# A two-layer graph kernel on one core: own place tables for each engine and batch, and a ring of 16 tiles

## The reference

```python
h = relu(layernorm(x))
# layer 0: 4 heads of 32, keys in 8 chunks of 128, softmax WITHIN each chunk
q, k, v = h @ Wq.T + bq, h @ Wk.T + bk, h @ Wv.T + bv
scores = where(adj == 0, -10, clip(q k^T / sqrt(32), -10, 10))   # adj as [row, chunk, key]
ctx = sum over chunks of softmax(scores in chunk) @ v_chunk
x = x + layernorm(ctx @ Wo.T + bo + h) * gamma + beta
# layer 1: graph attention
h = relu(layernorm(x)); Wh = h @ W
e = leaky_relu(Wh @ a1 (rows) + Wh @ a2 (columns)), -inf where adj == 0 off the diagonal
x = x + elu(softmax(e) @ Wh)
```

## Time and profile before

| | us |
|---|---|
| median of 3 runs | 904.6 (904.54 to 905.9) |
| the profiled execution | 901.52 |
| its span | 899.7 |
| DVE busy | 762.5 (85%) |
| PE busy | 750.4 (83%) |
| ACT busy | 593.6 (66%) |
| POOL busy | 512.3 (57%) |

### The profile page before, as it was taken

How to read it: one execution, slowest core, us unless ns; L and a number is a source line. 1 busy time by engine, 2 the same in 40 slices (tenths; PEclk the granted TensorE clock), 3 DMA queues, 4 the chain that set the end, 5 groups by cost and what they waited for, 6 DMA issues and landing times.

```text
span 899.7 us, 14629 instructions
## 1 busy us (share of the span) xinstructions
PE 750.4 (83%) x5031; PEld 429.3 (48%) x5031; DVE 762.5 (85%) x1348; ACT 593.6 (66%) x940; POOL 512.3 (57%) x478
## 2 busy tenths in 40 slices
PE   4799999988898998898899998898899887754644
PEld 2334444344454544464455545464356435644543
DVE  4877887898989988998989899998989896786783
ACT  6686787876867587767768676767865685235242
POOL 1301453463866667655866567755855487867443
PEclk9699999999999999999999999999999999766868
DMA  8413224202311223121321142121231201010101
GB/s 271 150 71 117 71 83 141 83 24 83 124 65 55 81 94 107 59 77 42 129 87 50 66 147 70 54 82 61 70 100 38 75 14 34 19 53 24 38 4 35
DMA packets 58648, 68.58 MB, mean 76 GB/s; under 512 B 5328, under 2 KB 35024, under 8 KB 58576
## 3 DMA queue, kind: packets, MB, share of 16 engines
q1 hardware_dynamic: 57568, 67.39, 22.3%
q10 hardware_dynamic: 1008, 0.26, 0.1%
HBM read 21.50 MB, written 12.58 MB: 38 GB/s over the span
## 4 chain that ended last, share of the span: by engine, by line
DVE 41%; PE 28%; issue 13%; ACT 9%; POOL 7%; DMA 1%; DVEq 0%; POOLq 0%; SPq 0%; ACTq 0%
DVE probs L854 14%; PE work L993 10%; DVE ring L756 6%; DVE ring L782 5%; PE ctx_ps L1035 4%; PE score L1022 4%; PE sum_ps L1041 4%; PE work L915 3%; DVE small L717 3%; DVE scaled L748 3%; ACT score L649 2%; POOL ring L464 2%; DVE small L722 1%; POOL h L494 1%; DVE inverse L832 1%
## 5 line engine op out<-in xcount | busy, mean ns | idle before, releaser
L854 DVE SCALAR_TENSOR_TENSOR probs<-score,cap 128x1024 f32<-128x1024 f32 x256 | 307.8, 1211 | 27.6 <-ACT score L649 27.4
L649 ACT ACTIVATE score<-score 128x1024 f32<-128x1024 f32 x256 | 257.5, 1011 | 61.5 <-PE score L1022 60.0
L514 POOL TENSOR_TENSOR gathered<-gathered,scaled 128x512 f32<-128x512 f32 x112 | 150.0, 1339 | 147.4 <-DVE scaled L748 147.4
L1022 PE MATMUL score<-query_stack,key_stack 128*128 128x512 f32 x512 | 190.6, 455 | 41.3 <-DVE probs L854 39.9
L464 POOL TENSOR_TENSOR ring<-ring,see_t 128x512 f32<-128x512 f32 x112 | 138.2, 1243 | 50.7 <-DVE ring L782 50.7
L993 PE MATMUL work<-wh,ring 128*128 128x129 f32 x1024 | 131.6, 288 | 40.0 <-ACT ring L572 38.4
L993 PEld LDWEIGHTS work<-wh,ring 128*128 128x128 f32 x1024 | 127.6, 204 | 48.8 <-issue 45.0
L1035 PE MATMUL ctx_ps<-probs,value 128*32 128x512 f32 x1024 | 137.7, 610 | 0.7 <-ACT context L657 0.7
L1041 PE MATMUL sum_ps<-probs,one_of 128*32 128x512 f32 x1024 | 135.1, 600 | 0.0
L782 DVE SCALAR_TENSOR_TENSOR ring<-near_row,wh,to_row 128x512 f32<-128x512 f32 x128 | 107.2, 853 | 27.3 <-ACT to_row L629 20.9
L1022 PEld LDWEIGHTS score<-query_stack,key_stack 128*128 128x128 f32 x512 | 79.5, 192 | 94.5 <-DVE probs L854 77.6
(11 more groups left out here) (99 smaller groups left out, 894.6 us busy)
## 6 DMA issues: line engine op xcount, KB each, us to landing
query_stack<-query_parts SPq DMA_DIRECT2D x64, 256.0 KB, 2.5
key_stack<-key_parts SPq DMA_DIRECT2D x64, 256.0 KB, 2.6
x_in<-in_x SPq DMA_DIRECT2D x16, 256.0 KB, 3.5
h_kept<-x_in SPq DMA_DIRECT2D x16, 256.0 KB, 2.0
res<-h_kept SPq DMA_DIRECT2D x16, 256.0 KB, 2.7
h<-in_x SPq DMA_DIRECT2D x16, 256.0 KB, 3.2
x_kept<-res SPq DMA_DIRECT2D x16, 256.0 KB, 2.6
gat_x<-x_kept SPq DMA_DIRECT2D x32, 128.0 KB, 2.3
```

What stands on the lines that cost most here:

```text
L514: nc.gpsimd.tensor_tensor(gathered[:, :, :], gathered[:, :, :], scaled[:, :, :], ALU.add).then_inc(gathered_step, 1)
L649: nc.scalar.activation(some, some, ACT.Exp, scale=DH ** -0.5).then_inc(exp_done, 1)
L854: nc.vector.scalar_tensor_tensor(out=probs[:, step[2] % 2, h:h + GROUP, :], in0=score[:, h:h + GROUP, :], scalar=LOW, in1=caps.broadcast_t ...
L1022: last = nc.tensor.matmul(score[:, head, :], key_stack[:, head, sc * P:(sc + 1) * P], query_stack[:, head, sq * HALF:(sq + 1) * HALF], sta ...
```

## The change

- The one table of slots is replaced by tables of places, one for each engine, and in them one for each batch: `in_order(engine)` sorts `b * 9600 + place` and each engine issues in that order. Every piece has a place of its own on each engine that has a part in it (a job on PE, its reading on ACT or DVE, its sum on POOL).
- The ring has 16 tiles. The wait in the middle of a batch's leaky pieces is gone; each half waits for the last shares of that half of the batch before.
- The peaks write their scratch output to `near_row` in place of ring tiles 6 and 7.
- Norms are cut in pieces (stats, moments, shift), ELU too (invert, divide, below, above), context and sums on PE as well, each with its own place.
- Masks: the turned adjacency and the second weights pass through the two `work` banks, not the `score` banks; the first half's `probs` waits for 4 masks only (`masks_made`), the second half's for 8.
- x is loaded and waited for by halves, and some semaphores are split by half.

What is computed and the kinds and sizes of the instructions stay as they are. The diff, cut to its core:

```diff
-RING = 12
+RING = 16
-JOBS = {
-    "turn_x0": -49, "turn_x1": -39, "query0": -29, "key0": -26, "value0": -20, ...
-}
-AT = {
-    "load_x": [-79], "moments_x": [-62, -57], "rstd_x": [-63, -57], ...
-}
+PLACES = 9600
+TENSOR = ({}, {
+    0: {
+        "scores": [-45, 13, 169, 668, 910, 1088, 1771, 1894, 2362, 2565, 2568, 2912, ...
+def table_of(engine, b):
+    return {**ENGINES[engine][0], **ENGINES[engine][1].get(b, {})}
+def in_order(engine):
+    found = [(b * PLACES + place, name, k, b) for b in range(BATCHES)
+             for name, places in table_of(engine, b).items() for k, place in enumerate(places)
+             if name != "hide" or here(engine, b, k)]
+    return [item[1:] for item in sorted(found, key=lambda item: item[0])]
...
-                        if step == (0, 0, 0):
-                            dve.wait_ge(masks_made, CHUNKS)
+                        if b == 0 and step % CHUNKS == 0:
+                            dve.wait_ge(masks_made, TILES * (step // CHUNKS + 1))
...
-                if n == RING:
-                    dve.wait_ge(work_done[bank_of("share1", g)], count_of("share1", g))
+                        if b:
+                            used = ("share", half * TILES + TILES - 1, b - 1)
+                            dve.wait_ge(work_done[bank_of(*used)], count_of(*used))
...
-                    out=ring[:, SCRATCH:SCRATCH + 2, :].rearrange("p a n -> p (a n)"), in0=to_row[:, :], in1=see[:, t, :],
+                        out=near_row[:, :], in0=to_row[:, :], in1=see[:, k, :], scale=1.0, scalar=-3e38, op0=ALU.add,
...
-                        last = nc.tensor.transpose(adj_turned_ps(t)[:, jt * P:(jt + 1) * P],
+                        last = nc.tensor.transpose(work[:, bank, :].bitcast(BF16)[:, jt * P:(jt + 1) * P],
```

More of the change, by code:

```diff
@@ new lines, with turn_of, bank_of @@
+IN_WORK = ("turn_x", "query", "key", "value", "gather", "turn_sums", "turn_context", "project", "turn_hidden", "to_row",
+           "wh", "near_row", "base_row", "share", "mask", "weights")
+TURNS = [item for item in in_order("tensor") if item[0] in IN_WORK and not (item[0] == "share" and item[1] % PAIR)]
+TURN_OF = {item: n for n, item in enumerate(TURNS)}
+def turn_of(name, k, b):
+    return TURN_OF[name, k // PAIR * PAIR if name == "share" else k, b]
+def bank_of(name, k, b):
+    return turn_of(name, k, b) % 2
@@ L96, in live, with count_of @@
+def count_of(name, k, b):
+    return turn_of(name, k, b) // 2 + 1
 def live(g):
     return 0 <= g < BATCHES
[L100 to L106, removed]
[L109 to L126 removed]
@@ L129, in step_at, with here @@
-def step_at(i, n, after):
-    i, n = i + (n - after) // SLOTS, (n - after) % SLOTS
-    return [(i, n // PHASE, n % PHASE // HEADS)] if n % HEADS == 0 and live(i) else []
-def group_at(i, n, places):
-    i, n = i + (n + places) // SLOTS, (n + places) % SLOTS
-    return [((i, n // PHASE, n % PHASE // HEADS), n % HEADS)] if n % GROUP == 0 and live(i) else []
-def group(step, h, plus=0):
-    i, q, c = step
-    return i * GROUPS + ((q * CHUNKS + c) * HEADS + h) // GROUP + plus
-def number(step, plus=0):
-    i, q, c = step
-    return i * STEPS + q * CHUNKS + c + plus
+def here(engine, g, n):
+    return (n in HIDE_HERE.get(g, ())) == (engine == "vector")
@@ L153, in build, with hidden, step_of, group_of @@
+def hidden(engine, g, n):
+    return sum(here(engine, f, t) for f in range(g + 1) for t in range(2 * CHUNKS if f < g else n + 1))
+def step_of(b, k):
+    return b * STEPS + k
+def group_of(b, k):
+    return b * GROUPS + k
 def build(nc, x, adj, Wq, bq, Wk, bk, Wv, bv, Wo, bo, gamma, beta, W, a, out):
@@ L721, in moments @@
                 for t in range(TILES):
-                    last = nc.vector.bn_aggr(moment[:, t, :], stats[:, t, :])
+                    last = nc.vector.bn_aggr(norm[s][1][:, t, :], norm[s][0][:, t, :])
                 last.then_inc(moments_done[s], 1)
@@ L969, in job @@
                         last = nc.tensor.matmul(work[:, bank, n * WIDE:(n + 1) * WIDE], h1_t[:, t * P:(t + 1) * P],
                                                 w1[:, :], start=True, stop=True)
-                elif name.startswith("to_row"):
-                    wait_read(f"turn_hidden{half}", b)
-                    last = nc.tensor.matmul(work[:, bank, :], w1_a[:, 1:2].broadcast_to([P, P]), h1_t[:, side],
-                                            start=True, stop=True)
-                elif name.startswith("near_row") or name.startswith("base_row"):
-                    pe.wait_ge(peak_done, b * 2 + 2)
-                    kind = int(name.startswith("base"))
-                    for t in range(TILES):
-                        tile = half * TILES + t
-                        last = nc.tensor.transpose(work[:, bank, t * P:(t + 1) * P],
-                                                   row_shift[:, kind, tile:tile + 1].broadcast_to([P, P]), eye[:, :])
-                else:
-                    assert name.startswith("share"), name
-                    pe.wait_ge(gat_exp_done, b * 2 * CHUNKS + CHUNKS * (half // 2 + 1))
-                    share(b, half, 0)
-                    return
@@ L987, in job @@
-                last.then_inc(work_done[bank], 1)
-            def share(g, k, part):
-                bank = bank_of(f"share{k}", g)
-                half, t = k // 2, k % 2 * PAIR + part
-                for jt in range(CHUNKS):
-                    last = nc.tensor.matmul(work[:, bank, part * (1 + D):(part + 1) * (1 + D)],
-                                            ring[:, (half * CHUNKS + jt) % RING, t * P:(t + 1) * P], wh[:, jt, 0:1 + D],
-                                            start=jt == 0, stop=jt == CHUNKS - 1)
-                if part == PAIR - 1:
-                    last.then_inc(work_done[bank], 1)
```

1796 lines of the change are left out of this document (1262 added, 534 removed), and 14 rows, old and new, of tables (JOBS, READ_AFTER).

## The result

The changed kernel takes **854.1 us** (median of 4 runs, 853.23 to 856.08) against 904.6 us (904.03 to 905.9): ratio 0.944, 95% interval 0.9424 to 0.9463. Forecast were 877 us and a range of 859 to 895. The direction was right and the size wrong: 50.5 us went, and 27.3 had been counted. Single runs of the kernel before lie between 897.6 and 906.1 us, the longer ones at the lower granted clock (0.956 at 897.6, 0.941 at 906.1).

What follows compares the result with a forecast made beforehand. DVE was taken to bound the full attention periods, PE close behind, and chains between engines the tail. Start -0.5, attention -4 and tail -22.8 sum to -27.3 us, giving 877 us, range 859 to 895.

Steps and rivals of the forecast that it cites:

- Start: Up to the first probs: little DVE work moves and masks share two work banks, -0.5 us, between -3 and +3.
- Attention: First to last probs: work moved in and new waits against two removed DVE waits, -4 us, between -18 and +12.
- DVE's two named waits: In the attention, DVE waiting for the ring of 12 (about 5 us) and for to_row (some 16 us).
- +7 of work moved in: Attention: leaky pieces, divides, a gather and a small piece now stand before the last probs, +7 us on DVE.
- -5 for the ring: Attention: with 16 tiles a tile is always free, so DVE's ring wait goes, -5 us.
- -9 of 16 for `to_row`: Attention, batches 2 to 7: some 16 us of DVE's to_row wait could go; -9 taken, as PE's transposes come later.
- +3: Attention: allowance of +3 us for new waits from a hundred moved pieces, not visible in the trace before.
- Tail: After the last probs: 127.6 us in place of 150.4, -22.8, between -29 and -12.
- Rival 3: Whole kernel: all named waits go, -18 us in the attention and -28 in the tail, 859 us; chance 0.12.
- Rival 1: Attention costs 12 us more than before, tail gives only 17; 900 us, for 888 to 903; chance 0.18.
- rival 2: Overlapped periods: PE's in-order queue becomes the bound, +38 us, so 920 us and slower; chance 0.06.
- Rival 4: Tail: PE's clock could stay at 2.4 GHz, 3 us less, 874 us; chance 0.11.

Runs made afterwards that it cites:

- experiment 5: Changed kernel with sums rejoined to context products, aggregates to statistics, and row_shift late, each alone and all three together: 870.1, 860.9, 861.3 and 883.9 us.
- `row_shift_late`: Changed kernel with row_shift of batches 0 to 5 moved to two probs ahead of the first leaky piece on DVE: 861.3 us.
- `old_after_b0`: Changed kernel's code, with the engines' order of before from batch 1's beginning on: 897.3 us, ratio 0.993 to the kernel before.
- `before_leaky_late`: Kernel before with 16 ring tiles and the first leaky piece two slots later, the third and first hide one slot later: 901.8 us, ratio 0.998.
- experiment 1: Changed kernel's code with old order from first probs, from batch 1, up to last probs only, or in the tail only: 900.8, 897.3, 901.1, 858.4 us.
- `old_sums_spread`: Changed code in the old order from the first probs on, but sums of 59 steps set apart as in the new order: 936.9 us.
- `old_order`: Changed kernel's code, 16 tiles and start, with the order of before from the first probs on: 900.8 us, ratio 0.998 to the kernel before.
- `sums_joined`: Changed kernel with sums put directly behind the context products of their step on PE, as before: 870.1 us.
- `new_sums_all_apart`: Changed kernel with sums of 68 of the remaining 69 steps also moved further back on PE: 884.2 us.
- `before_ring16`: Kernel before with a ring of 16 tiles and nothing else: 897.3 us, ratio 0.993.

## Why the prediction was wrong, step by step

- **Start** (-0.5, in -3 to +3): measured -1.8. That no mask is strewn was right, all eight still stand ahead of the first `probs`.
- **Attention** (-4, in -18 to +12): measured -28.0. **This is the step that failed**: the attention was added up from DVE's two named waits, "7 - 5 - 9 + 3", and its lower end was "all idle of this kind gone". What moved was PE's waiting for DVE (`score<-probs` 39.9 to 12.8, `row_shift` 8.4 to nothing) and DVE's busy time (9 us less for the same work), neither of which had a term. Undoing three parts of the order, none of which brought back a wait that the forecast had counted, cost 29.8 us (experiment 5). The named waits taken alone, over the whole kernel, were worth 4 to 7 us for the ring (897.3 for 904.2) and nothing for `to_row`. The bound was wrong in kind: 66.8 us of PE's idle time and 74.3 of DVE's lay in the attention, and an order can take from either.
- In the figures of single terms: the +7 of work moved in is there (DVE 1113 instructions for 1100), -5 for the ring was 2.6 at most between the two profiled runs of the old order, -9 of 16 for `to_row` has nothing behind it (that wait gained nothing in the old order, and `row_shift_late` brought back PE's wait and not this one), and where +3 stood for new waits, `scaled` (+6.6) and `inverse` (+2.5) make 9.1.
- **A term missed**: batch 0's period fell from 64.4 to 61.0 us. Before, PE's granted clock fell to 0.50 at its start, after it had been busy 1.70 of 5 us with the masks. Stretches of before, and then of after:

```profile
25.00:30.00 5.00, 1.70 (x21) 1.39 (x22) 4.93 (x12) 3.17 (x4) 0.00 (x0) 0.81 0.86 281
30.00:35.00 5.00, 4.09 (x12) 2.09 (x9) 3.93 (x8) 3.43 (x4) 1.91 (x5) 0.50 0.01 2
35.00:40.00 5.00, 4.33 (x16) 1.60 (x20) 3.78 (x4) 2.26 (x4) 4.29 (x12) 0.50 0.57 210
```
```profile
25.00:30.00 5.00, 3.75 (x37) 3.06 (x37) 5.00 (x12) 4.16 (x9) 0.00 (x0) 1.00 1.00 331
30.00:35.00 5.00, 2.44 (x9) 1.24 (x7) 4.98 (x13) 2.80 (x4) 0.00 (x0) 1.00 0.31 88
```

  The new start has PE busy 3.75 us there, and in this run the clock stays at 2.4 GHz. It need not: in `old_after_b0`, with the same start and batch 0 and the same 3.75 and 2.44 us, the clock fell to 1.2 GHz for 3.4 us (0.66 granted over 35 to 40). No run was made for the clock, but kept traces part the 3.4 us. Batch 0 of `before_leaky_late`, whose order there is that of before, and of `old_after_b0`, whose order there is the new one:

```profile
34.60:96.70 62.10, 58.57 (x376) 23.92 (x380) 48.09 (x63) 46.87 (x65) 14.20 (x23) 1.00 0.26 92
```
```profile
32.60:94.90 62.30, 59.75 (x363) 22.86 (x364) 52.05 (x80) 49.63 (x72) 21.39 (x33) 0.97 0.27 97
```

  The old order took 64.4 us at a granted clock of 0.94 and 62.1 at 1.00; the new one 62.3 at 0.97 and 61.0 at 1.00. So 2.3 of the 3.4 us go with the clock and 1.1 with batch 0's order, by one run each.
- **Tail** (-22.8, in -29 to -12): measured -17.8, and its steps can be followed. DVE and PE in order of time, and below them the times after the last `probs` (719.5):

```profile
722.98 0.96 DVE L1438 RECIPROCAL inverse<-work 128x128 f32<-128x128 f32 x1 [2.24 <-PE work L1567]
725.10 1.74 DVE L1476 CUSTOM_DVE_ANT_0 near_row<-to_row,see 128x1024 f32<-128x1024 f32 x1 [1.16 <-ACT to_row L1310]
...
751.72 0.75 DVE L1503 SCALAR_TENSOR_TENSOR ring<-near_row,wh,to_row 128x512 f32<-128x512 f32 x1 [0.83 <-ACT near_row L1320]
...
795.92 1.23 DVE L1476 CUSTOM_DVE_ANT_0 near_row<-to_row,see 128x1024 f32<-128x1024 f32 x1 [1.77 <-ACT to_row L1310]
...
810.93 5.20 DVE L1503 SCALAR_TENSOR_TENSOR ring<-near_row,wh,to_row 128x512 f32<-128x512 f32 x5 [2.53 <-ACT near_row L1320]
...
818.88 0.68 DVE L1508 TENSOR_TENSOR ring<-ring,see_t 128x512 f32<-128x512 f32 x1
...
835.23 1.52 DVE L1508 TENSOR_TENSOR ring<-ring,see_t 128x512 f32<-128x512 f32 x1
```
```profile
757.28 1.09 PE L1567 MATMUL work<-eye,h 128*128 128x128 f32 x4 [3.69 <-ACT h L1247]
...
792.67 0.60 PE L1567 MATMUL work<-eye,h 128*128 128x128 f32 x4
```

| after the last `probs` | forecast | measured |
|---|---|---|
| inverse sums | 4 | 3.5 |
| batch 6's first peak | 5.5 | 5.6 |
| batch 6's first leaky piece | 28 | 32.2 |
| batch 7's half 0 turned | 32 | 37.8 |
| batch 7's first peak | 68 | 76.4 |
| batch 7's first leaky piece | 87 | 91.4 |
| from there to the end | 40.3 | 41.2 |

  Batch 7's chain is 8.4 us later than forecast (beyond the 75 named as a sign of being wrong), since its halves come one behind the other and each of the steps before ran 4 to 6 us late; 4.0 us came back at the peaks (15.0 us to the first leaky piece where 19 had been taken over from before). Yet the cause given for the gain was only half right: the order in the tail did not do it, the attention's did (experiment 1).
- **Rivals.** Rival 3 ("all waits named go", 859) came nearest and fell short too. Against it stood "PE at 90% can't follow a period below some 94 us without gaps". PE does follow 90.9 us at 97%. Rival 1 (888 to 903) and rival 2 (a slower kernel through PE's queue) did not happen here, though `old_sums_spread` shows that an order can do that: 36 us for the places of 59 pieces. Rival 4: the tail's clock rose from 0.76 and 0.75 in its two stretches to 0.79 and 0.77, no more.
- **The signs named.** Periods of 97 to 99 us for batches 3 to 6 were named, and came out as 92.3, 90.9, 93.1 and 95.6. No `to_row` wait in the attention, no stop at the ring: both seen.

**What stays open.** 20 of the 50.5 us are not put down to a part of the order; the engines' orders were not taken over one at a time. Nor are the 29.8 us of the three parts a sum that the old order would gain from them: there the sums' places alone cost 36. How much of POOL's 17 us is shorter DVE pieces was not separated. Why the ring of 16 is worth 4 to 7 us in the old kernel and, with masks and start, only 3 in `old_order` is not known. Why PE is busier when sums stand apart, and what in the new order makes the distance of 59 sums a gain, was not settled.

## What to carry to other kernels

When two engines are both above 85% busy and feed each other, read the waits of both, and bound a change of order by the idle time of the busier one in that stretch: here PE's 66.8 us (it was busy 648.1 us in the attention, DVE 640.6), not DVE's two waits of 20. A named wait need not be worth its length: of three taken away or put back here, one gained nothing (`to_row`, 16.0 us), one some 4 to 7 us (the ring, 6.4 long) and one 7.2 (PE's for `row_shift`, 8.1 long). Take it away in the old kernel before counting it. To learn which engine a kernel pays for, add a little work to each in turn and read the price of a microsecond.

## What the runs showed of the hardware that was not expected

- Instructions issued in a row overlap: 192 statistics with a mean of 0.277 us each added 35 to 39 us of busy time and not 53, and 512 transposes with a mean of 0.28 us added 48 to 53 us.
- The same 5031 matmuls kept PE busy for 740.0 us in `sums_joined`, 749.0 in the changed kernel and 763.3 in `new_sums_all_apart`: the order alone moves PE's busy time by 3%.
- Batch 0's attention in the old order took 64.4, 63.5 and 62.1 us at a granted clock of 0.94, 0.97 and 1.00 (`before`, `before_ring16`, `before_leaky_late`).
- Cutting POOL's two wide instructions to 64 columns took 32 us off DVE's busy time in the attention, with DVE's own instructions as they were.
